# Rows of negated maxima: one small product, a copy and a DMA instead of eight transposes and two row copies

## What is computed

```python
def attn(h):                                   # 16 heads of 32, causal
    q, k, v = (heads(h @ w.T + b) for w, b in ((q_w, q_b), (k_w, k_b), (v_w, v_b)))
    scores = einsum('bhqd,bhkd->bhqk', q, k) / sqrt(32)
    scores = where(ki > qi, -inf, scores)
    return merge(softmax(scores) @ v) @ o_w.T + o_b

x = x + layernorm(attn(layernorm(x)))
gate, up = split(layernorm(x) @ w_gate_up.T)   # 2 x 2048
x = x + layernorm((silu(gate) * up) @ w_down.T)
```

## Time and profile before

| | |
|---|---|
| median of 3 runs | 1105.98 us (1105.91 to 1109.69) |
| profiled execution | 1108.12 us |
| its span on the core | 1106.3 us, mean granted TensorE clock 0.964 of full |
| busy, share of the span | TensorE 93%, VectorE 62%, GpSimd 56%, ScalarE 37% |
| attention | about 84 to 506 us, with the projection stage of the first batch between units 7 and 8 |

### The profile page before, as it was taken

How to read it: one execution, slowest core, us unless ns; L and a number is a source line. 1 busy time by engine, 2 the same in 40 slices (tenths; PEclk the granted TensorE clock), 3 DMA queues, 4 the chain that set the end, 5 groups by cost and what they waited for, 6 DMA issues and landing times.

```text
span 1106.3 us, 16499 instructions
## 1 busy us (share of the span) xinstructions
PE 1025.9 (93%) x5792; PEld 794.9 (72%) x5792; DVE 685.3 (62%) x1216; ACT 409.4 (37%) x651; POOL 617.0 (56%) x348
## 2 busy tenths in 40 slices
PE   3889999997989999896889999899998999989996
PEld 2667777775877777654678888688886888868885
DVE  6666887785787778843854544644456545564454
ACT  3216665563146555542232322322233222322221
POOL 4106878898237887886444554445453544535450
PEclk9989999998999999967989999999999999999998
DMA  6313333334213233211423223332324223242330
GB/s 212 100 50 84 82 80 77 92 87 124 68 39 82 73 96 76 60 39 59 139 88 107 92 86 113 134 113 85 111 88 161 87 92 107 86 161 85 112 106 38
DMA packets 52505, 104.32 MB, mean 94 GB/s; under 512 B 10848, under 2 KB 10848, under 8 KB 52192
## 3 DMA queue, kind: packets, MB, share of 16 engines
q1 hardware_dynamic: 52448, 103.59, 30.2%
HBM read 70.00 MB, written 8.39 MB: 71 GB/s over the span
## 4 chain that ended last, share of the span: by engine, by line
PE 78%; DVE 12%; POOL 4%; ACT 2%; issue 2%; DMA 2%; SPq 1%; DVEq 0%; ACTq 0%; POOLq 0%
PE ps L1101 19%; PE ps L1103 18%; PE ps L1102 18%; PE ps L1185 7%; PE ps L1157 6%; PE ps L1219 5%; POOL p_sum L588 2%; PE ps L1233 1%; PE ps L1168 1%; DVE h_lo L981 1%; DMA x_in<-x 1%; DVE xt_lo L877 1%; PE ps L1193 1%; DVE p_sum L863 1%; DVE stats L1073 1%
## 5 line engine op out<-in xcount | busy, mean ns | idle before, releaser
L604 POOL TENSOR_TENSOR gu_lo<-gu_raw,gu_hi 128x1024 fp32r<-128x1024 f32 x64 | 154.2, 2410 | 275.8 <-ACT gu_hi L786 275.8
L900 DVE CUSTOM_DVE_ANT_0 ps<-ps,mask_q 128x384 f32<-128x384 f32 (+7 forms) x256 | 190.1, 777 | 38.1 <-PE ps L1157 35.2
L1101 PE MATMUL ps<-xt_hi,gu_hi 128*128 128x512 f32 x512 | 200.6, 392 | 0.0
L1102 PE MATMUL ps<-xt_lo,gu_hi 128*128 128x512 f32 x512 | 200.1, 391 | 0.0
L1103 PE MATMUL ps<-xt_hi,gu_lo 128*128 128x512 f32 x512 | 200.0, 391 | 0.0
L975 DVE TENSOR_TENSOR h<-ps,silu 128x512 f32<-128x512 f32 x64 | 44.2, 690 | 246.9 <-PE ps L1103 246.9
L981 DVE TENSOR_TENSOR h_lo<-h,h_hi 128x512 fp32r<-128x512 f32 x64 | 159.9, 2499 | 2.2
L1185 PE MATMUL ps<-q_stack,k_stack 98*128 98x512 f32 (+3 forms) x384 | 116.4, 386 | 4.1 <-DVE q_stack L919 1.7
L786 ACT ACTIVATE gu_hi<-gu_raw 128x1024 fp32r<-128x1024 f32 x64 | 67.9, 1061 | 139.3 <-PE ps L1103 113.4
L1101 PE MATMUL ps<-dn_hi,h_hi 128*128 128x512 f32 x256 | 102.9, 402 | 14.9 <-DVE h_lo L981 11.6
L1157 PE MATMUL ps<-k_stack,q_stack 96*128 96x512 f32 (+3 forms) x384 | 111.2, 366 | 5.2 <-DVE m_full L900 2.8
(11 more groups left out here) (121 smaller groups left out, 1802.3 us busy)
## 6 DMA issues: line engine op xcount, KB each, us to landing
gu_raw<-gu_w SPq DMA_DIRECT2D x64, 512.0 KB, 3.6
dn_raw<-dn_w SPq DMA_DIRECT2D x64, 256.0 KB, 2.7
x_in<-x SPq DMA_DIRECT2D x32, 256.0 KB, 4.2
q_stack<-st_hi SPq DMA_DIRECT2D x128, 64.0 KB, 2.0
k_stack<-st_hi SPq DMA_DIRECT2D x128, 64.0 KB, 2.0
qk_raw<-qk_w SPq DMA_DIRECT2D x16, 256.0 KB, 3.0
q_stack<-st_lo SPq DMA_DIRECT2D x64, 64.0 KB, 2.0
k_stack<-st_lo SPq DMA_DIRECT2D x64, 64.0 KB, 2.0
```

The source lines that it names most:

```text
L604: nc.gpsimd.tensor_tensor(gu_lo[:, s], gu_raw[:, s], gu_hi[:, s].bitcast(F32), ALU.subtract).then_inc(gu_split, 1)
L900: nc.vector.tensor_tensor_reduce(out=scores, in0=scores, in1=mask_q[:, SEQ - (t + 1) * P:], scale=1.0, scalar=MASKED, op0=ALU.add, op1=ALU ...
L1101: nc.tensor.matmul(dst, hi, r_hi, start=start, stop=False)
L1102: nc.tensor.matmul(dst, hi, r_lo, start=False, stop=False)
```

## The change

`negated` now writes its parts side by side into `m_cols`, a new tile of 128 x 32 in fp32r (first the high, then the low parts, head by head). One fp32r product with `m_cols` as weights and an identity `ident_r` as moving data turns it into 32 rows of 128 in one PSUM bank. VectorE copies these 32 x 128 numbers to slot 4 of `x_in`. One DMA, issued by ScalarE, takes them into rows 96 and 97 of `q_stack` for both heads. The first scores wait for this DMA. `ident_r` is one more copy on GpSimd at the start. In the order of TensorE, the second quarter of the projection moves ahead of the product, the late values behind it, and the fourth quarter ahead of the first scores.

```diff
-        m_spread = x_in[:, 4, 0:TT * M_STEP].rearrange("p (t n) -> p t n", n=M_STEP)
+        m_rows = x_in[0:2 * 2 * TT, 4, P:2 * P]
...
+            nc.gpsimd.tensor_copy(ident_r[:, :], ident[:, :]).then_inc(pool_hi, 1)
+            pool.wait_ge(pool_hi, 9)
...
-            def max_rows(g):
-
-                use = use_of_rows(g)
-                act.wait_ge(bank_full, use + NCH)
-                first = use % RING * CH
-                nc.scalar.activation(q_stack[QK_ROWS:ROWS, g % 2, 0], ps_cols[0:2, first:first + SEQ], ACT.Copy).then_inc(m_rows0, 1)
+            def load_maxima(g):
+
+                act.wait_ge(m_copied, g + 1)
+                to = q_stack[QK_ROWS:ROWS, g % 2].rearrange("p h (t n) -> p (h t) n", n=P)
+                act.dma_start(to.bitcast(F32), m_rows).then_inc(m_loaded, DMA)
 
             def body(g):
                 projected = g + 2 < ALL_UNITS
+                load_maxima(g)
                 if g % UNITS:
                     copy_acc(g - 1)
-                max_rows(g)
...
-                negative = ps[:, use % RING, 0:2 * TT].rearrange("p (t h) -> p t h", h=2)
-                m_hi, m_lo = m_spread[:, :, 0:HD + 1:HD].bitcast(F32R), m_spread[:, :, 1:HD + 2:HD].bitcast(F32R)
-                nc.vector.tensor_scalar(negative.bitcast(F32R), m_full[:, :, :], -1.0, None, ALU.mult).then_inc(dve_unit, 1)
+                negative = ps[:, use % RING, 0:2 * TT].rearrange("p (h t) -> p h t", h=2)
+                m_hi, m_lo = (m_cols[:, n * 2 * TT:(n + 1) * 2 * TT].rearrange("p (h t) -> p h t", h=2) for n in range(2))
+                m = m_full.rearrange("p t h -> p h t")
+                nc.vector.tensor_scalar(negative.bitcast(F32R), m, -1.0, None, ALU.mult).then_inc(dve_unit, 1)
...
             def max_rows(g):
 
                 use = use_of_rows(g)
                 vec.wait_ge(bank_full, use + NCH)
-                first = use % RING * CH
-                nc.vector.tensor_copy(q_stack[QK_ROWS:ROWS, g % 2, 1], ps_cols[HD:HD + 2, first:first + SEQ]).then_inc(bank_free, NCH)
+                if g:
+                    vec.wait_ge(m_loaded, DMA * g)
+                nc.vector.tensor_copy(m_rows, ps[0:2 * 2 * TT, use % RING, 0:P]).then_inc(m_copied, 1)
+                vec.wait_ge(m_copied, g + 1)
+                vec.sem_inc(bank_free, NCH)
...
-                for t in range(TT):
-                    at_col = use % RING * CH + t * P
-                    last = nc.tensor.transpose(ps_cols[:, at_col:at_col + P], x_in[:, 4, t * M_STEP:t * M_STEP + P], ident[:, :])
-                last.then_inc(bank_full, NCH)
+                nc.tensor.matmul(ps[0:2 * 2 * TT, use % RING, 0:P], m_cols[:, :], ident_r[:, :], start=True, stop=True).then_inc(bank_full, NCH)
...
                 if r == 0:
-                    pe.wait_ge(m_rows0, g + 1)
-                    pe.wait_ge(bank_free, use_of_rows(g) + NCH)
+                    pe.wait_ge(m_loaded, DMA * (g + 1))
...
-                project_next(0, 0)
+                project_next(0, 0, 1)
+                transpose_maxima(g)
                 if has_sums(g):
                     values(g - 1, LATE_VALUES)
-                transpose_maxima(g)
-                project_next(0, 1)
+                project_next(0, 2)
                 maxima_of_next(0)
-                project_next(0, 2)
-                maxima_of_next(1)
-                pe.wait_ge(m_rows0, g + 1)
-                maxima_of_next(2)
+                project_next(0, 3)
+                maxima_of_next(1, 2)
                 scores(g, 0)
-                maxima_of_next(3)
-                project_next(0, 3)
-                maxima_of_next(4, 5)
+                maxima_of_next(3, 4, 5)
                 scores(g, 1)
```

More of the change, by code:

```diff
@@ L88 @@
 assert sorted(m[:2] for m in MAXES) == [(h, t) for h in range(2) for t in range(TT)]
-M_STEP = 48
 MAX_OFF = [sum(m[2] for m in MAXES[:n]) for n in range(len(MAXES))]
@@ L274, in build @@
             ident = sb(att, "ident", [P, P])
+            ident_r = sb(att, "ident_r", [P, P], F32R)
+            m_cols = sb(att, "m_cols", [P, 2 * 2 * TT], F32R)
             ident_bf = sb(att, "ident_bf", [P, P], BF16)
@@ L337, in build @@
         m_ready = sem("m_ready")
-        m_rows0 = sem("m_rows0")
+        m_copied = sem("m_copied")
+        m_loaded = sem("m_loaded")
         score_full = sem("score_full")
@@ L553, in _ @@
             pool.wait_ge(consts_made, 2)
-            made = [8]
+            made = [9]
             def split(hi, lo, raw, done):
@@ L906, in negated @@
                 vec.wait_ge(bank_free, use)
-                negative = ps[:, use % RING, 0:2 * TT].rearrange("p (t h) -> p t h", h=2)
-                m_hi, m_lo = m_spread[:, :, 0:HD + 1:HD].bitcast(F32R), m_spread[:, :, 1:HD + 2:HD].bitcast(F32R)
-                nc.vector.tensor_scalar(negative.bitcast(F32R), m_full[:, :, :], -1.0, None, ALU.mult).then_inc(dve_unit, 1)
+                negative = ps[:, use % RING, 0:2 * TT].rearrange("p (h t) -> p h t", h=2)
+                m_hi, m_lo = (m_cols[:, n * 2 * TT:(n + 1) * 2 * TT].rearrange("p (h t) -> p h t", h=2) for n in range(2))
+                m = m_full.rearrange("p t h -> p h t")
+                nc.vector.tensor_scalar(negative.bitcast(F32R), m, -1.0, None, ALU.mult).then_inc(dve_unit, 1)
                 vec.wait_ge(dve_unit, g + 1)
                 nc.vector.tensor_copy(m_hi, negative).then_inc(m_ready, 1)
-                nc.vector.scalar_tensor_tensor(m_lo, m_full[:, :, :], -1.0, negative, ALU.mult, ALU.subtract).then_inc(m_ready, 1)
+                nc.vector.scalar_tensor_tensor(m_lo, m, -1.0, negative, ALU.mult, ALU.subtract).then_inc(m_ready, 1)
             def max_rows(g):
```

## The result

The changed kernel takes 1109.82 us (median of 20 executions, 1106.82 to 1113.81), the kernel before 1107.25 us (median of 20 beside them); the ratio is 1.0024, 95% interval 1.0012 to 1.0035. It is slower by 2.7 us, between 1.3 and 3.9; forecast were 2.8 us and 1108.8. One of the 20 executions of before took 2549.52 us; the ratio leaves it out.

What follows compares the result with a forecast made beforehand. TensorE's instruction order was taken to pace each unit. Twelve full units +3.5 us, unit 8 -0.6, unit 0 +0.1, units 14 and 15 -0.2 gave +2.8 on a median of 1105.98: 1108.8 us, range 1103 to 1114.

Steps and rivals of the forecast that it cites:

- The stall: TensorE waiting for VectorE's last negated maxima before the new product, which starts 0.05 us after that write; 0.76 us per full unit.
- E: Moment when VectorE's last write of the negated maxima ends in a unit; 195.62 us in unit 5 before the change.
- Two signs: Before the product in full units: idle time put down to VectorE, and 0.7 to 0.8 us idle of weight loading.
- full units: Attention units 1 to 7 and 9 to 13, forecast at +0.29 us each, +3.5 us for the 12.
- The product: The fp32r product replacing eight transposes on TensorE (0.84 us); taken as 0.13 us, between 0.05 and 0.32.
- First scores: TensorE's first scores of a unit: 4.1 to 4.2 us after E, released by TensorE's own order, not by the transfer.
- The exponentials bind: Second half of the second scores waits for ScalarE's first exponentials, no longer hidden under the fourth quarter: +0.29 us per full unit.
- Distance: Time from one full unit to the next: 22.7 us forecast instead of 22.41.
- The term of the other units: Units that are not full: unit 8 -0.6 us, unit 0 +0.1, units 14 and 15 together at most -0.2.
- The late transfer: Rival: the new DMA, moving rows through few engines, lands after 3.43 us and delays first scores; 1123 us, chance 0.14.
- The faster rival: Rival: VectorE finishes the maxima 0.7 us earlier, no stall opens; -0.47 us per full unit, 1099.7 us, chance 0.12.
- The clock: Rival: idle stretches make TensorE's clock fall; one more fall gives 1112 us, one in each unit 1150; chance 0.07.

## Why the prediction was right, step by step

The measured time is 1.0 us above the forecast of 1108.8 because the kernel before took 1107.25 beside it and not 1105.98; the change itself, 2.7 against 2.8, is what the steps below are about.

**The stall**: forecast 0.76, the product starting 0.05 after E. Measured: the second quarter would end at 193.92 + 0.70 = 194.62, the product starts at 195.43, 0.81. That the stall costs was shown by filling it. Two signs came otherwise: the profile puts the idle time down to "issue" and not to VectorE in the full units, and weight loading idles 1.06 us there, not 0.7 to 0.8.

**The product**: forecast 0.13. Measured 0.15 with the late values behind it, and it stays at 0.15 to 0.18 in the two kernels without a stall that have values behind it. With a projection behind it, it is 0.06 to 0.09, after a stall (unit 8) as without one. So what it costs goes with what follows it, not with the stall.

**First scores**: forecast 4.18 after E, measured 4.25; the transfer hidden, as forecast, with 1.3 us to spare where I had allowed 3.43 - 2.0. From product to issue are 196.00 - 195.43 = 0.57 us, not 0.70: the 0.30 and the 0.10 in that sum stood on no row, and the product's result reached VectorE's copy in 195.69 - 195.43 = 0.26.

**The exponentials bind**: forecast second half 1.73 after the first scores, measured 201.30 - 199.58 = 1.72. Column sums forecast 6.44, measured 6.53. Distance forecast +0.29, measured +0.37. The excess of 0.08 is mainly the stall's 0.05 and the product's 0.02.

**The term of the other units** was mis-sized. Unit 8: forecast -0.6, measured 21.07 - 21.39 = -0.32. Its first scores come only 0.08 earlier and not 0.27, since the transfer takes 2.27 and not 2.0; and the second half of the second scores is 1.82 behind them and not 1.73, since the first exponential starts 0.69 behind scores that have waited for the DMA and 0.58 behind others. Unit 0: forecast +0.1, measured 22.20 - 21.70 = +0.5; its first scores wait for the transfer too. Units 14 and 15: forecast at most -0.2, from first scores 2.75 after E in unit 14. They came at 4.47, at half the clock, and still unit 14 alone is -1.26, by another place of the clock falls.

From E of unit 0 to E of unit 15 the sum is 400.25 - 397.32 = +2.9 us in the profiled executions, against +2.8 forecast; this agreement is partly luck, since errors cancel. The 12 full units give +4.0 and not 3.5: +2.2 in units 1 to 6, +0.5 in unit 7 with the stage behind it, +1.3 in units 9 to 13. It is less than 12 x 0.37 = 4.4 because units 9 and 13 of before were 22.65 and 22.59 us long. Unit 0 adds 0.5, units 8 and 14 take 0.3 and 1.3 off.

**What stays open.** From E of unit 15 on both profiled executions of the changed kernel are 2.0 us shorter, and they come to unit 0 earlier (E at 82.03 and 83.35 against 84.30 and 83.88), so that their spans (1105.0 and 1106.0) lie at or under those of before (1106.3 and 1106.0), while the medians over 20 say +2.6. These two have a mean clock of 0.972 and 0.971; of the 20 executions timed only three reach 0.97, the first of the two among them, and most of the others have 0.966 to 0.968. So it may be that most executions lose more to the low clock than the profiled ones. It is not shown: three of the 20 took only 1106.9 to 1107.3 us at 0.966 and 0.967, and no trace here is of an execution as long as the median. The cost of the full units repeats and is shown. That the medians differ by just what the attention loses is not shown, and may be luck in part.

**The late transfer**: its mechanism is there. The Trainium skill's rule (DMA: Bandwidth & Descriptors, section "Why a DMA increments its semaphore by 16 and not by 1") gave two engines, and the queue of ScalarE bears it out:

```profile
q10 hardware_dynamic: 544, 0.26, 0.1%
```

544 packets in 16 transfers are 34 each: 32 of 512 B and two of 4 B, which I read as one completion for each of two engines. The updates of the transfer's semaphore fit that: in unit 5 one comes 1.07 us after the issue and then two more, at 2.21 and 2.23. But the price was wrong. From issue to use it is 2.27 us, against a landing after 2.0 for the 64 KB copies, so 0.3 more at most, not 1.2. The step that failed in this rival is the price of a packet: 0.086 us was the mean of unit 4, where 924 of 1324 packets have 2 KB or more. In unit 5 all 34 packets fall into 0.6 us, from 197.2 to 197.8:

```profile
q10 hardware_dynamic: 34, 0.02, 9.6%
```

That is 0.096 x 16 x 0.6 / 34 = 0.027 us each, 0.43 for 16 in a row.

**The faster rival** failed as argued: the microsecond freed on VectorE and ScalarE turned into waiting (VectorE waits 2.66 us for the first maximum, ScalarE 3.94 for the values), and E stayed where it was, 2.10 us behind the start of the first quarter against 2.11 before. **The clock**: no fall in any full unit, with 0.67 us idle in each; in unit 14, with 2.04 us, there was one.

## What to carry to other kernels

Before work is moved ahead of or behind a wait, count what it covered: here eight transposes became one product, five to ten times shorter, and a stall of 0.81 us, opened by moving the values, took the place of what they had cost. Look for the same thing one step on: an operation between two dependent steps of another engine (the quarter between the scores) is cover too. And when the end of some work releases large DMAs, check which small one they will then be ahead of.

## What the runs showed of the hardware that was not expected

- ScalarE issues a DMA while its own copy runs: both start at 203.56. It is not free: the operation behind the copy starts 0.73 to 0.77 us after the copy's start instead of 0.49.
- A small fp32r product (32 weight columns, 128 moving) holds TensorE 0.06 to 0.09 us with a projection behind it and 0.15 to 0.18 with the late values behind it; eight fp32 transposes 0.79 to 0.85 and 1.03. With a projection behind, and for the product with the values behind too, a stall ahead changes nothing.
- A 16 KB transfer issued 0.45 us behind two loads of 512 KB takes 4.70 us to be used, instead of 2.27.
- The clock falls repeat from one execution to the next of the same kernel in places (468.0 and 467.8 us in the profiles of before, 459.5 and 460.6 in those of the changed kernel), and differ in others (the second profile of the changed kernel has one more, from 68.0 to 71.4 us).
- One and the same code took 21.55 and 24.08 us (unit 0), 21.86 and 25.69 (unit 14), by where the granted clock was at half.
